# Cross-attention and feed-forward layer on one core: first context loaded and multiplied in parts, statistics of block 0's norm tiles behind DVE's 7th to 10th query copies

## What is computed

```python
def reference(x, ctx, itok, W_kvc, W_dq, W_uq, W_qr, W_uk, W_kr, W_uv, W_o, gate_w, up_w, down_w, gate_s, up_s, down_s):
    q = layernorm(x)                               # 16 x 100 x 512
    kv_c = ctx @ W_kvc                             # 512 -> 128
    q_c = q @ W_dq                                 # 512 -> 192
    q_nope, q_rope = q_c @ W_uq, rope(q_c @ W_qr)  # 16 heads x 128, x 64
    k_nope, v, k_rope = kv_c @ W_uk, kv_c @ W_uv, rope(kv_c @ W_kr)
    scores = (q_nope . k_nope + q_rope . k_rope) / sqrt(192)
    attn = softmax(where(itok - 8 <= key <= itok, scores, -1e30))
    x = x + (attn @ v) @ W_o
    h = silu((layernorm(x) @ gate_w.T) * gate_s) * ((layernorm(x) @ up_w.T) * up_s)
    return x + (h @ down_w.T) * down_s
```

## Time and profile before

| | us |
|---|---|
| median of 3 runs | 760.04 |
| lowest and highest | 757.87, 764.9 |
| the profiled execution, whole | 759.56 |
| its span, first to last instruction | 757.8 |
| PE busy in the span | 714.1 |
| DVE, ACT, POOL busy | 442.1, 395.7, 200.2 |

### The profile page before, as it was taken

How to read it: one execution, slowest core, us unless ns; L and a number is a source line. 1 busy time by engine, 2 the same in 40 slices (tenths; PEclk the granted TensorE clock), 3 DMA queues, 4 the chain that set the end, 5 groups by cost and what they waited for, 6 DMA issues and landing times.

```text
span 757.8 us, 17572 instructions
## 1 busy us (share of the span) xinstructions
PE 714.1 (94%) x6970; PEld 664.7 (88%) x6970; DVE 442.1 (58%) x940; ACT 395.7 (52%) x886; POOL 200.2 (26%) x330
## 2 busy tenths in 40 slices
PE   4999898999998999999999999989999999999997
PEld 4888778779987998779987899779899999999996
DVE  2999836754566536755467446767463545536242
ACT  5888744673457535674357535688382323323130
POOL 1656855604063312604054301630000000000000
PEclk9999999999999999999999999999999999999999
DMA  8999754244314433044313442039111212020111
GB/s 282 344 378 314 267 154 98 63 92 89 98 28 109 89 70 88 19 124 88 92 37 111 90 83 72 3 122 373 36 36 36 71 36 69 6 79 18 36 54 35
DMA packets 46363, 81.28 MB, mean 107 GB/s; under 512 B 5482, under 2 KB 30106, under 8 KB 46282
## 3 DMA queue, kind: packets, MB, share of 16 engines
q1 hardware_dynamic: 40796, 53.67, 26.5%
q0 software_dynamic: 5488, 26.50, 10.2%
HBM read 57.26 MB, written 11.28 MB: 90 GB/s over the span
## 4 chain that ended last, share of the span: by engine, by line
PE 73%; DVE 9%; DMA 6%; ACT 5%; issue 3%; SPq 2%; POOL 1%; DVEq 0%; POOLq 0%
PE ps L1461 17%; PE ps L1169 13%; PE ps L1021 11%; PE ps L1499 8%; PE ps L1174 6%; PE ps L1097 4%; DMA kv_table<-tab 4%; PE ps L1070 3%; PE ps L194 3%; ACT q_lat L1207 2%; SPq L921 2%; PE ps L1032 2%; PE ps L1061 2%; PE ps L1086 1%; PE ps L844 1%
## 5 line engine op out<-in xcount | busy, mean ns | idle before, releaser
L1311 DVE TENSOR_TENSOR o_parts<-q_lat,o_parts 128x320 fp32r<-128x320 f32 x80 | 68.2, 870 | 67.6 <-ACT o_parts L1215 67.6
L1169 PE MATMUL ps<-o_parts,wvo_hi 128*128 128x320 f32 x320 | 96.8, 313 | 1.8 <-ACT o_parts L1215 1.8
L1169 PE MATMUL ps<-o_parts,wvo_lo 128*128 128x320 f32 x320 | 95.7, 310 | 0.0
L1215 ACT ACTIVATE o_parts<-q_lat 128x320 fp32r<-128x320 f32 x80 | 63.9, 821 | 45.0 <-PE ps L1169 44.9
L1546 ACT ACTIVATE silu<-ps,ffn_scale 128x320 f32<-128x320 f32 x55 | 29.0, 527 | 97.5 <-PE ps L1461 96.9
L959 POOL TENSOR_TENSOR rot_c<-gathered,cosq 128x192 f32<-128x192 f32 x40 | 25.0, 624 | 162.8 <-PE ps L1032 150.3
L1594 DVE SCALAR_TENSOR_TENSOR hidden<-ps,ffn_scale,silu 128x320 f32<-128x320 f32 x55 | 30.2, 549 | 61.2 <-ACT silu L1546 54.9
L1169 PEld LDWEIGHTS ps<-o_parts,wvo_hi 128*128 128x128 f32 x320 | 60.6, 189 | 2.3 <-ACT o_parts L1215 2.0
L1169 PEld LDWEIGHTS ps<-o_parts,wvo_lo 128*128 128x128 f32 x320 | 60.4, 189 | 0.3
L1174 PE MATMUL ps<-o_parts,wvo_hi 128*128 128x320 f32 x320 | 60.1, 309 | 0.0
L538 PE MATMUL ps<-wkv,ctx_hi 128*128 128x384 f32 x192 | 52.7, 384 | 5.1 <-ACT ctx_hi L402 5.1
(11 more groups left out here) (167 smaller groups left out, 1747.2 us busy)
## 6 DMA issues: line engine op xcount, KB each, us to landing
ctx_raw<-ctxT_dram SPq DMA_DIRECT2D x16, 722.0 KB, 9.1
gathered<-key_rows SPq DMA_DIRECT2D x240, 47.2 KB
head_w<-head_w_dram SPq DMA_DIRECT2D x16, 576.0 KB, 7.8
ffn_raw<-ffn_w_dram POOLq DMA_DIRECT2D x11, 768.0 KB, 12.9
kv_table<-tab POOLq DMA_DIRECT2D x16, 288.0 KB, 6.6
rows<-x_dram SPq DMA_DIRECT2D x5, 640.0 KB, 5.2
residual<-x_dram SPq DMA_DIRECT2D x20, 160.0 KB, 2.3
x_rows<-residual SPq DMA_DIRECT2D x20, 160.0 KB, 2.0
```

The source lines that it names most:

```text
L1169: last = pe.matmul(ps[:, 4 + m, 0:TB], w[wt][:, h, cols], o_hi[h % RING], start=(h == 0 and n == 0), stop=False, skip_group_check=True)
L1215: act.activation(o_hi[h % RING], q_lat[:, h % 2, :, h // 2], ACT.Copy).then_inc(oh_ok, 1)
L1311: dve.tensor_tensor(o_lo[h % RING], q_lat[:, h % 2, :, h // 2], o_hi[h % RING].bitcast(F32), ALU.subtract).then_inc(ol_ok, 1)
```

## The change

There are two parts. In the first, context 0 alone is loaded by two DMAs of two chunks each, the first with a semaphore of its own, `first_front_half`. ACT waits for the first half before chunk 0 and for the second before chunk 2. DVE makes the low part of context 0 chunk by chunk, each as soon as ACT's copy of it has raised `sums`, and then that of the means: five instructions in place of one. PE starts the high products of context 0 as soon as the first chunk is there; its order changes from tile by tile to chunk by chunk for the tiles 0 and 1, which hold no columns of the means, and tile 2 comes last, after `ctx_hi`. The other 15 contexts are handled as before. In the second part the tuple of the statistics depends on the block: in block 0 they follow the copies of queries 13, 15, 17 and 19, in the others those of 3, 9, 15 and 21.

```diff
@@ sync
-            load_ctx(0)
+            sp.dma_start(raw[0][:, 0:2, 0:LK], a["ctxT"][0, :, 0:2]).then_inc(front_half, 16)
+            sp.dma_start(raw[0][:, 2:4, 0:LK], a["ctxT"][0, :, 2:4]).then_inc(ctx_in[0], 16)
@@ scalar
-                act.wait_ge(ctx_in[i], 16 * (n // RAWS + 1))
+                if n == 0:
+                    act.wait_ge(front_half, 16)
+                else:
+                    act.wait_ge(ctx_in[i], 16 * (n // RAWS + 1))
                 if n >= 2:
                     act.wait_ge(mm, n - 1)
                 for c in range(KC):
+                    if n == 0 and c == 2:
+                        act.wait_ge(ctx_in[0], 16)
@@ vector
+            def first_low_context():
+
+                for c in range(KC):
+                    dve.wait_ge(sums, c + 1)
+                    dve.tensor_tensor(lo[0][:, c, 0:LK], raw[0][:, c, 0:LK], hi[0][:, c, 0:LK].bitcast(F32),
+                                      ALU.subtract)
+                dve.wait_ge(ctx_hi, 1)
+                dve.tensor_tensor(lo[0][:, :, LK:LK + MEANS], raw[0][:, :, LK:LK + MEANS],
+                                  hi[0][:, :, LK:LK + MEANS].bitcast(F32), ALU.subtract).then_inc(ctx_lo, 1)
...
+            first_low_context()
             for n in range(NB):
-                low_context(n)
                 if n:
+                    low_context(n)
                     table_sum(n - 1)
@@ tensor
+            def first_table_high():
+
+                for c in range(KC - 1):
+                    pe.wait_ge(sums, c + 1)
+                    for t in range(KT - 1):
+                        high(0, t, c)
+                pe.wait_ge(ctx_hi, 1)
+                for c in range(KC - 1):
+                    high(0, KT - 1, c)
+
             for n in range(NB - 1):
-                table_high(n)
+                if n:
+                    table_high(n)
+                else:
+                    first_table_high()
@@ attention, vector
-        adds, stats = (5, 7, 13, 17), (3, 9, 15, 21)
+        adds = (5, 7, 13, 17)
+
+        def stats(first):
+            return (13, 15, 17, 19) if first else (3, 9, 15, 21)
...
-                if o in stats:
-                    next_norm(b, last, stats.index(o))
+                if o in stats(first):
+                    next_norm(b, last, stats(first).index(o))
```

More of the change, by code:

```diff
@@ L274, in build_setup @@
             sem(s) for s in ("mm", "part_ev", "tab_sum", "rope_c", "rope_s", "tab_done"))
+        front_half = sem("first_front_half")
         tab_out = fetch.written
```

## The result

The changed kernel takes 751.51 us (median of 4 executions, 750.62 to 751.84), the kernel before 759.76 us beside it (757.87 to 764.9): a ratio of 0.9873, 95% interval 0.9839 to 0.9906. The forecast was 756.3, with a range from 752.6 to 760.0. In two later comparisons the changed kernel gave 0.9871 (0.9850 to 0.9892) and 0.9852 (0.9803 to 0.9902).

The account below looks back on a forecast made before the run. PE, busy 94% of the span, was taken as the bound, so only its waits or slow stretches pay. 3.54 (stall) + 0.2 (start) = 3.7 us, giving 755.9, or 756.3 against the median; range 752.6 to 760.0.

Parts of the forecast that it names:

- the sizing of the stall: Block 0, PE idle before query 9 until block 1's token rows land: removing this gains 3.54 us, bounds 1.5 and 3.6.
- So the stall cost its 3.54 us and nothing on top: Behind PE's idleness before query 9: clock stayed at 1.00 through 112 to 116, so no slow stretch to win back.
- The start: First context in halves and chunks: PE begins 2.8 us earlier, of which 0.2 us remains; bounds -0.6 and +2.8.
- context 1 stays the limit: Setup's start: context 1's load is not split, so ACT's high part stays near 15.6 and DVE's low part too.
- a new wait of PE for DVE at 24.9: Setup's start: PE would wait 1 to 2 us for DVE's low part of context 2.
- the waits for the writes of the tables: Setup's loop: DVE waits five times before 108 us, 4.3 us in all; part of the start's gain is lost there.
- The start's lead survives: Rival: PE's earlier start lasts through setup; gain up to 6.3 us, time 753.7, chance 0.1.
- The clock falls less: Rival: slow stretches in 96 to 100 and 416 to 424 vanish; 3.3 us more gained, time 753.0, chance 0.03.
- The stall is replaced: Rival, block 0: other waits take back some 2 us and the start gives nothing; gain 1.5, time 758.5, chance 0.13.
- the three: Block 0: token rows, key rows or POOL might come late by some 2 us of the 3.54.
- DVE's pairs: Block 0: four copies each followed by a statistic, each pair leaving 0.20 us idle, so no copy late, cost 0.
- the margin of 2.4 us for the token rows: Block 0: rows landed by 114.14, moved statistics due near 116.6, so 2.4 us to spare.

Follow-up runs that it names:

- the first execution: The kernel before, nothing changed: the profiled execution that the prediction read, 759.56 us.
- filling products: Kernel before, PE running 30 products that nobody reads ahead of query 9 of block 0: 760.32 us, ratio 0.9970; with 44: 759.96 us, 0.9966.
- the second profile of before: The kernel before run once more, nothing changed: 765.6 us (one execution).

## Why the prediction was wrong

- **The step that failed is the sizing of the stall.** "The stall costs 4.28 - 0.74 = 3.54 us" is the right reading of one execution, and it was taken as the term of the sum with an upper bound of 3.6. The stall is not a duration, it is a difference: the landing of a load that SP issues in its own time, less PE's arrival. Counted from SP's first issue of key rows both vary by about 2 us, and in the first execution both stood on the favourable side. The term measured 7.95 us (761.11 - 753.16) and 7.5 (761.95, the median of the executions of before that the ratio uses, less 754.41); by the ratios it is 6.6 and 10.1, and 8.6 in the profiles of block 0. The hint stood in the earlier trace rows: a slow stretch in 96 to 100, just ahead of the stall, which in that execution cost nothing, since PE would have waited for the rows anyway. What is hidden by a wait has to be added to it when the wait is removed; this follows from the profiles, no run took it apart.
- **"So the stall cost its 3.54 us and nothing on top" failed too.** In 112 to 116 the clock was at 1.00 behind 3.29 us of idleness. In the six other profiles with an unfilled wait, of 4.59 to 6.12 us, it fell each time, at a cost of some 2.5 us. The rule of the Trainium skill that the prediction weighed and set aside (TensorE: Matmul & The Clock Gate, "Why this matters for your kernels": no idle gaps between bursts of matmuls) had it right for this place; one row could not refute it.
- **The start: 0.2 forecast, about 2 us measured** where the stall is gone, inside the bounds (-0.6 to 2.8). The mechanism was right in all its steps (context 1 stays the limit, DVE gains only its wait for ACT, a new wait of PE for DVE at 24.9), and the size was read from the profile of nine in which this wait was shortest: 0.49 us where the others have 0.66 to 1.83. Where the rest, up to the 2.5 us of the first query product, comes from is seen at table sum 5 but was not taken apart. That the waits for the writes of the tables would take the rest back was wrong in six of the eight profiles.
- **The rivals.** "The start's lead survives" (753.7, chance 0.1) had the right direction for half of the reason. "The clock falls less" (753.0, chance 0.03) was right in kind and put it in the wrong place. The mean of 1 less the granted clock, times the span, is 8.3 to 9.7 us in five comparisons of before (95 executions) and 3.9 to 4.6 us in three of the changed kernel: 4 to 5 us less of slow clock, of which about 2.5 us is the stretch behind the stall. The rest was not taken apart: the other slow stretches, near 50, 160, 240, 410, 500 and 540 us, come and go from profile to profile. "The stall is replaced" did not come: PE waited for none of the three, and DVE's pairs left the 0.20 us. But the margin of 2.4 us for the token rows was 0.8 us in one profile of the changed kernel and about nothing in two, since SP issues them later behind the first query product than in the execution that was read.
- **Do the terms add up?** 7.5 to 8 us for the second part and 2 for the first make about 10 us. The three ratios of the changed kernel (0.9873, 0.9871, 0.9852) stand for 9.7 to 11.3 us of 761, its three medians for 8.3, 10.0 and 9.8.
- **The range** was narrow because each bound came from the same execution as its term. The times of before scattered over 7 us (757.87 to 764.9), which said that some of its waits differ between executions; the prediction left that scatter out of the range instead of asking which waits they are.

## What to carry to other kernels

A stall that ends with a transfer from an independent queue has the length landing less arrival. Before it goes into a sum, look at what stands right ahead of it: a wait or a slow stretch there shortens it in this execution, and comes back when it is removed. A second profile of the unchanged kernel would have told here more than any row of the first. And add to a wait of PE of several us the slow products behind it, unless rows of several executions show none.

## What the runs showed of the hardware

The clock behind an idle PE: 1.00 behind 3.29 us in one profile, 0.50 to 0.61 behind 4.59 to 6.12 us in six, 0.58 behind 2.28 us that followed 4.56 us of filling products, and 1.00 throughout where 44 products filled the whole wait. (The values are means over the 4 us behind the wait, or over the last of it.) At the end of the setup, waits of 1.86 and 2.09 us were followed by 0.61 and 0.69 over 96 to 100, waits of 1.94 and 1.70 us by 1.00. So the length of the gap alone does not decide it.

At the very start the column of the granted clock is 1.00 while the products run at about half speed. In the second profile of before four low products of context 0 take 1.00 us at 15.04 and again at 16.21, and 0.64 us at 17.39:

```profile
12.02 3.22 PE L538 MATMUL ps<-wkv,ctx_hi 128*128 128x384 f32 x9 [5.09 <-ACT ctx_hi L402]
15.04 1.00 PE L555 MATMUL ps<-wkv,ctx_lo 128*128 128x192 f32 x4
...
16.21 1.00 PE L555 MATMUL ps<-wkv,ctx_lo 128*128 128x192 f32 x4
...
17.39 0.64 PE L555 MATMUL ps<-wkv,ctx_lo 128*128 128x192 f32 x4
```

```profile
12.00:16.00 4.00, 3.98 (x14) 4.00 (x15) 2.14 (x2) 2.53 (x10) 0.00 (x0) 1.00 1.06 364
```

In the first profile the same group took 0.58 us already at 15.05. The speed of the first products is to be read from their spacing, and it differs between executions by more than the 0.49 us on which the start's term was built.
